# A three-stage attention kernel: new slot tables for all stages, three masks instead of four on TensorE, and whole-width first fills

## The reference

```python
# layer 0: grouped convolution (8 heads, kernel 3) makes q, k, v
scores = einsum('bhdl,bhdm->bhlm', qh, kh) / sqrt(8) - 1e9 * mask      # 8 heads, 256 keys, causal
x = layernorm(softmax(scores) @ vh + swapaxes(q_in))                   # B=128, L=256, C=128
# layer 1 (self) and layer 2 (keys and values from ctx): 16 heads of depth 16, 128 keys
logits = einsum('bhqd,bhkd->bhqk', qh, kh) / 4 + mask * -1e9
out = layernorm(x + (softmax(logits) @ vh) @ wo + bo)
# feed-forward 256 -> 1024 -> 256 with relu, residual and layernorm
```

## Time and profile before

| | us |
|---|---|
| median of 3 runs | 4481.46 (4481.1 to 4481.8) |
| the profiled execution | 4476.52 |
| its span on the core | 4474.7 |
| PE busy in the span | 4144.4 (93%) |
| DVE busy | 3523.3 (79%) |
| ACT, POOL busy | 3136.7 (70%), 2872.4 (64%) |

### The profile page before, as it was taken

How to read it: one execution, slowest core, us unless ns; L and a number is a source line. 1 busy time by engine, 2 the same in 40 slices (tenths; PEclk the granted TensorE clock), 3 DMA queues, 4 the chain that set the end, 5 groups by cost and what they waited for, 6 DMA issues and landing times. The chain is left out here.

```text
span 4474.7 us, 129562 instructions
## 1 busy us (share of the span) xinstructions
PE 4144.4 (93%) x46216; PEld 3376.6 (75%) x46216; DVE 3523.3 (79%) x13839; ACT 3136.7 (70%) x6279; POOL 2872.4 (64%) x4568
## 2 busy tenths in 40 slices
PE   7999999999999969999999986999999997999999
PEld 5777777777777747777777765788787776999998
DVE  7898988989988859999999985777777774555555
ACT  5777777777777748888888875777777775444443
POOL 4777777777776637777777764766766762444444
PEclk9999999999999979999999998999999998999999
DMA  5444444444444436767777756898889882222221
GB/s 137 119 125 119 123 123 120 125 120 122 122 121 123 114 94 154 169 160 172 162 165 170 162 131 144 195 197 193 194 197 193 194 184 90 71 71 71 71 71 53
DMA packets 1082953, 608.79 MB, mean 136 GB/s; under 512 B 64664, under 2 KB 1082056, under 8 KB 1082312
## 3 DMA queue, kind: packets, MB, share of 16 engines
q1 hardware_dynamic: 1071896, 595.70, 54.8%
q10 hardware_dynamic: 10416, 4.80, 0.5%
HBM read 175.66 MB, written 117.54 MB: 66 GB/s over the span
## 5 line engine op out<-in xcount | busy, mean ns | idle before, releaser
L1142 DVE CUSTOM_DVE_ANT_0 l_junk<-l_bank,mask 128x256 bf16<-128x256 f32 x2048 | 776.8, 418 | 47.6 <-PE l_bank L830 33.7
L995 ACT ACTIVATE mha_probs<-mha_bank 128x512 f32<-128x512 f32 x1024 | 611.3, 601 | 278.9 <-DVE mha_bank L1157 154.0
L995 ACT ACTIVATE l_probs<-l_bank 128x512 f32<-128x512 f32 x1024 | 604.6, 597 | 266.2 <-DVE l_bank L1157 258.8
L1157 DVE TENSOR_TENSOR l_bank<-l_bank,mask0t 128x512 f32<-128x512 f32 x768 | 530.5, 691 | 25.9 <-PE l_bank L862 22.4
L1142 DVE CUSTOM_DVE_ANT_0 mha_junk<-mha_bank,mask 128x128 bf16<-128x128 f32 x2048 | 462.3, 284 | 29.7 <-PE mha_bank L830 29.4
L830 PE MATMUL l_bank<-l_stack 96*128 96x256 bf16 x2048 | 385.2, 274 | 58.8 <-DMA l_stack<-l_parts 29.6
L830 PE MATMUL mha_bank<-mha_stack 96*128 96x128 bf16 (+1 forms) x4096 | 355.8, 221 | 79.2 <-DVE mha_max_parts L1142 48.0
L1557 ACT ACTIVATE ffn_hidden<-ffn_h,ffn_b_s 128x512 f32<-128x512 f32 x256 | 176.4, 689 | 354.8 <-PE ffn_h L1504 344.1
L862 PE MATMUL l_bank<-l_stack 99*128 99x128 bf16 x4096 | 403.1, 221 | 9.7 <-ACT l_probs L995 4.3
L1157 DVE TENSOR_TENSOR mha_bank<-mha_bank,mask1t 128x512 f32<-128x512 f32 x512 | 354.9, 693 | 71.2 <-PE mha_bank L862 66.1
L862 PE MATMUL mha_bank<-mha_stack 99*128 99x128 bf16 (+1 forms) x4096 | 395.8, 220 | 15.4 <-DMA mha_stack<-mha_max_rows 13.6
(11 more groups left out here) (197 smaller groups left out, 11430.0 us busy)
## 6 DMA issues: line engine op xcount, KB each, us to landing
mha_stack<-mha_parts SPq DMA_DIRECT2D x1536, 128.0 KB, 3.5
l_stack<-l_parts SPq DMA_DIRECT2D x1024, 64.0 KB
l_stack<-l_parts SPq DMA_DIRECT2D x256, 128.0 KB
rows_o<-mha_resid SPq DMA_DIRECT2D x64, 512.0 KB, 3.5
cols_o<-mha_y_t SPq DMA_DIRECT2D x128, 256.0 KB, 3.0
l_x_pad<-in_x SPq DMA_DIRECT2D x64, 256.0 KB, 3.3
l_c_pad<-in_ctx SPq DMA_DIRECT2D x64, 256.0 KB, 3.2
l_resid<-in_x_t SPq DMA_DIRECT2D x64, 256.0 KB, 3.2
```

Of the source, the lines that this page charges most:

```text
L995: nc.scalar.activation(probs[:, i % RING, :], tbank[i % 2][:, :], ACT.Exp).then_inc(att_exp, 1)
L1142: ins = nc.vector.tensor_tensor_reduce(out=junk[:, i % 2, cols], in0=sbank[i % 2][:, cols], in1=mask, scale=1.0, scalar=LOWEST, op0=ALU.ad ...
L1157: nc.vector.tensor_tensor(bank_, bank_, mask.unsqueeze(1).to_broadcast([P, 4, P]), ALU.add).then_inc(att_masked, 1)
```

## The change

It has three parts.

1. The slot tables of all three stages are new. In stage 0 a fourth mask (chunk 15) moves from PE to DVE, the scores come mostly one slot later, and both halves of the values are done whole in slot 0 and slot 2. In stage 1 score chunks 2 and 4 are one slot later and the second values are done whole in slot 5. In stage 2 the scores start two slots later and end in slot 18 instead of 16, the turn of the heads moves from slot 4j+5 to 4j+6, the turn of maxima of half 1 from slot 3 to slot 5 and that of half 0 from slot 9 to slot 12, the last projection from slot 11 to slots 11 and 12, one turn of y from slot 7 to slot 9, and `split_slot` from 14 to 13.
2. The first unit of each stage fills its stack by transfers over all 512 tokens: half as many of them, each twice as large. Its first score waits for all of them.
3. The counts of the semaphores follow.

```diff
 stage 0:
-        score=[2, 3, 4, 6, 7, 8, 10, 10, 11, 12, 12, 13, 14, 14, 15, 16],
+        score=[3, 4, 5, 7, 7, 8, 10, 10, 11, 12, 12, 13, 14, 15, 16, 18],
-        pe_masks=(4, 12, 14, 15),
+        pe_masks=(4, 12, 14),
-        work=[((0, 1), 'values', 1, 0),
+        work=[((0,), 'values', 1, 0),
-              ((9,), 'turn_y', -1, 3),
+              ((8,), 'turn_y', -1, 3),
-              ((13,), 'turn_y', 0, 0),
+              ((12,), 'turn_y', 0, 0),
 stage 1:
-        score=[4, 4, 6, 8, 8, 9, 11, 12, 12, 13, 13, 14, 15, 15, 17, 18],
+        score=[4, 4, 7, 8, 9, 9, 11, 12, 12, 13, 13, 14, 15, 15, 17, 18],
-              ((5, 6), 'values', 1, 1),
+              ((5,), 'values', 1, 1),
 stage 2:
-        score=[2, 2, 4, 4, 6, 6, 8, 8, 11, 11, 12, 13, 13, 14, 15, 16],
+        score=[4, 4, 5, 7, 8, 8, 9, 9, 10, 10, 12, 13, 13, 14, 15, 18],
-        steps={'turn': 5, 'turn_merged': 7, 'output': 8, 'normalise': 9},
-        dve_steps={'recip': (5, 1), 'merge': (5, 2), 'low': (7, 1), 'add': (8, 1), 'stats': (8, 1), 'moments': (9, 0), 'epsilon': (9, 1)},
+        steps={'turn': 6, 'turn_merged': 7, 'output': 8, 'normalise': 9},
+        dve_steps={'recip': (5, 1), 'merge': (5, 1), 'low': (6, 2), 'add': (8, 2), 'stats': (8, 2), 'moments': (9, 1), 'epsilon': (9, 1)},
         work=[((0,), 'values', 1, 0),
-              ((1,), 'values', 1, 1),
-              ((3,), 'max', 0, 1),
-              ((3, 4), 'project', 2, 0),
+              ((2,), 'values', 1, 1),
+              ((3,), 'project', 2, 0),
+              ((5,), 'max', 0, 1),
               ((6,), 'turn_y', -1, 2),
               ((7,), 'project', 2, 1),
-              ((7,), 'turn_y', -1, 3),
+              ((9,), 'turn_y', -1, 3),
               ((9,), 'project', 2, 2),
-              ((9,), 'max', 1, 0),
-              ((11,), 'project', 2, 3),
+              ((12,), 'max', 1, 0),
+              ((11, 12), 'project', 2, 3),
-        split_slot=14,
+        split_slot=13,
 the fills:
+        def fill_first(u, side):
+            fill_side(u, slice(0, 4 * P), stack_in[0][side], side)
```

More of the change, by code:

```diff
@@ L80 @@
         split_lag=0,
-        pool_steps={'power': (9, 0)},
+        pool_steps={'power': (9, 2)},
         work=[((0,), 'turn_y', -1, 1),
@@ L578, in attention, with filled @@
     FILLED = len(FILLS) + (1 if phase == 2 else 0)
+    FIRST_FILLED = [sum(sides[-1] == side for _, _, sides in FILLS) + (1 if phase == 2 and side == 0 else 0)
+                    for side in range(2)]
+    def filled(u, half):
+        return 16 * (FILLED * u.k + (FIRST_FILLED[half] if u.par == 0 else FILLED))
     def place(side, h):
@@ L680, in load_resid, with fill_side @@
                          res_units[u.u]).then_inc(resid_ld[u.par], 16)
-        def fill_side(u, half, side):
-            tokens = slice(2 * half * P, 2 * (half + 1) * P)
-            if side == 0:
-                wait(sp, att_mm, CHUNKS * (u.u - 2) + 8 * (half + 1) if u.number() not in (0, 1) else 0)
-                if phase == 2:
-                    sp.dma_start(stack[STACK:SCORED, u.par, side_of((1,)), tokens],
-                                 mask2_units[u.u][:, tokens].unsqueeze(1).to_broadcast([3, H, 2 * P])
-                                 ).then_inc(stack_in[u.par][half], 16)
+        def fill_side(u, tokens, signal, side):
+            if phase == 2 and side == 0:
+                sp.dma_start(stack[STACK:SCORED, u.par, side_of((1,)), tokens],
+                             mask2_units[u.u][:, tokens].unsqueeze(1).to_broadcast([3, H, tokens.stop - tokens.start])
+                             ).then_inc(signal, 16)
             wait(sp, split_done, projected(u, GROUPS * (side + 1) - 1))
@@ L695, in fill_side @@
                                  parts[:, u.par, GROUPS * sides[0]:GROUPS * (sides[-1] + 1), part, tokens]
-                                 ).then_inc(stack_in[u.par][half], 16)
+                                 ).then_inc(signal, 16)
+        def fill_first(u, side):
+            fill_side(u, slice(0, 4 * P), stack_in[0][side], side)
         def fill_stack(u, half):
-            fill_side(u, half, 0)
-            fill_side(u, half, 1)
+            wait(sp, att_mm, CHUNKS * (u.u - 2) + 8 * (half + 1) if u.number() != 1 else 0)
+            for side in range(2):
+                fill_side(u, slice(2 * half * P, 2 * (half + 1) * P), stack_in[u.par][half], side)
         def store(u):
@@ L737, in slots @@
             if t.number() == -2:
-                for half in range(2):
-                    fill_side(t.plus(2), half, 0)
+                fill_first(t.plus(2), 0)
             yield
@@ L747, in slots @@
             if t.number() == -2:
-                for half in range(2):
-                    fill_side(t.plus(2), half, 1)
+                fill_first(t.plus(2), 1)
             elif exists(t.plus(2), N):
@@ L822, in score_step @@
             if i % 8 == 0:
-                pe.wait_ge(stack_in[u.par][i // 8], 16 * FILLED * (u.k + 1))
+                for half in range(2) if u.number() == 0 else (i // 8,):
+                    pe.wait_ge(stack_in[u.par][half], filled(u, half))
             if i == 0 and phase == 2 and u.number() == 0:
@@ L959, in project_out @@
                 for half in range(2):
[L960 removed]
+                    act.wait_ge(stage1[f"stack_in0{half}"], c["stage1_filled"][half])
             if i == 0:
                 for half in range(2):
[L963 removed]
+                    wait(act, stack_in[u.par][half], filled(u.plus(-2), half))
             args = {"scale": SCALE if side == 0 else 1.0}
@@ L1373, in attention @@
         c["stage1_values"] = work_count(Unit(N // 2 - 1, 1), "values", VSTEPS - 1)
-        c["stage1_fills"] = 16 * FILLED
+        c["stage1_filled"] = [filled(Unit(N // 2 - 1, 0), half) for half in range(2)]
     return dict(n=N, sync=sync_program, tensor=tensor_program, scalar=scalar_program, vector=vector_program,
```

6 lines of the change are left out of this document (2 added, 4 removed).

## The result

| | before | after |
|---|---|---|
| median of 4 runs | 4481.63 (4481.1 to 4482.28) | 4563.55 (4558.58 to 4567.76) |
| the profiled execution | 4476.52 | 4558.58 |
| its span | 4474.7 | 4556.8 |
| mean granted clock | 0.985 | 0.974 |

The changed kernel is slower: ratio 1.0182, 95% interval 1.0165 to 1.02, 82 us. The forecast was 4542 us, with a range of 4455 to 4605. "0 to 1" is the distance from the first exponential of stage 0's last unit to that of stage 1's first.

What follows compares the result with a forecast made beforehand. PE's list was taken as the path in stages 0 and 2, PE and DVE bounding each other in stage 1. Terms -30 + 0 - 10 + 101 = +61 us, on 4476.5 plus 4.9, gave 4542 us; range 4455 to 4605.

Steps and rivals of the forecast that it cites:

- The cover from the rows of before: Stage 2: PE's work between the turn of maxima of half 1 and attend 8, 3.27 us after 8.84 before.
- the transfer (5.5): Stage 2: time from ACT's issue of the maxima transfer to attend 8, taken as 5.5 us, near the loaded rows.
- The wait forecast, 2.95 us a unit: Stage 2: new wait of PE at attend 8 for the transfer of maxima, 31 times, +91 us in all.
- The case of 6.08 us: Stage 2: slowest traced issue-to-attend time, which the prediction placed in the last unit; worst-case wait 3.53 us.
- The turn of the heads' wait: Stage 2: PE's 0.48 us wait at this turn goes, since it comes two slots behind the freeing output; -15 us.
- +0.4 us for each of the two: Stage 2: PE's waits for maxima (0.69 us) and normalisation (0.60 us) each grow by 0.4 us, 25 us together.
- a rival with 20%: Stage 2: the clock falls in each unit behind the wait, costing 1.7 us of PE's time, 53 us: 4595; chance 20%.
- Two matmuls off PE, 35.8 us less: Stage 0: leaving chunk 15's mask off PE saves 0.56 us in each of 64 units, 35.8 us.
- The fills' wait, 21.2 us: Stage 0: PE's 21.2 us of waiting for stack fills goes, since the first score comes one slot later.
- nothing else on PE changes its count there: Stage 0: apart from the mask's two matmuls, PE's work keeps its count; the stage's forecast was -30 us.
- DVE did not become the bound: Stage 0 rival: DVE, 0.69 us more a unit, becomes the bound; stage 0 +22 instead of -30, 4594; chance 12%.
- until SP gets to its end: Barrier into stage 2: PE stands still 16.70 us for SP's queue; issuing 13 instead of 26 saves 8.5 us.
- The other steps of PE and ACT are long done: Barrier into stage 2: no other chain ends later than SP's issues, so the 8.5 us less counts in full.

Runs made afterwards that it cites:

- experiment 4: Changed kernel, each of the 24 fills of stage 2's later units moving a quarter of its rows (32 KB instead of 128 KB): 4451.14 us, ratio 0.9935.
- Experiment 3: Changed kernel with ten further, unused matmuls of 512 columns on PE ahead of attend 8's wait for the maxima in stage 2: 4515.52 us, ratio 1.0083.
- experiment 9: Changed kernel with stage 2's old table, plus chunk 15's mask back on PE: 4465.05 us; or instead stage 0's turn of y back in slot 13: 4447.73 us.

## Why the prediction was right, and where it was wrong

**Stage 2, the transfer: right, both as cause and as size.** The cover from the rows of before (3.27 us) was 3.39, the turn to the issue (0.72) was 0.77, and the transfer (5.5) was 5.2. The wait forecast, 2.95 us a unit, is 2.6 to 2.7. The choice near the loaded end was the one that mattered, and experiment 4 shows its reason, the fills around it. (The case of 6.08 us that it leaned on is the last unit but one, with twelve fills around it, and not the last.) The Trainium skill's rule ("DMA: Bandwidth & Descriptors", section "Anatomy of one DMA — SWDGE (gpsimd) path"), an estimate of 2.06 us for 24 KB, is stated for one DMA on GpSimd's path, and this one goes from ACT's queue. No transfer that PE waited for in stages 1 and 2 was that fast in any trace: the shortest took 2.45 us, and 2.9 was the median with few bytes.

**Stage 2, the other waits.** The turn of the heads' wait went (-0.48), as forecast. The step that failed is "+0.4 us for each of the two": each time that it occurs, the wait for maxima went from 0.69 to 0.73 us and the one for the normalisation from 0.60 to 0.55. That PE's halt at attend 8 gives DVE time is not the reason, since in experiment 4, where the halt is gone, they are 0.74 and 0.55 (21.4 us in 29 and 15.3 us in 28 cases). The new order has the room that the forecast denied it; the 0.8 us a unit did not come.

**The clock.** It stood as a rival with 20% and 1.7 us a unit, in place of nothing in the sum. Experiment 3 measures 1.41 us. So the forecast of +3.27 a unit met +3.37 by luck, in offsetting errors: 0.8 us for waits that did not grow and a transfer's wait 0.3 us too large stood in for 1.4 us of clock. By experiment 3 the sum is 1.96 (32.30 - 30.34: the new wait less the old one of the heads) and 1.41. The argument against the rival, that no wait of the steady stages was over 1.5 us, said only that the trace of before could not show it; the step that failed is that it then put the clock at nothing in the sum.

**Stage 0.** -30 was forecast and -21 came, but not by its steps. "Two matmuls off PE, 35.8 us less" failed: experiment 9 gives 3 us for it. The rest, 18.7 us (1530.8 to 1512.1), comes with four masks still on PE. The fills' wait, 21.2 us, is gone there as forecast, but a wait of 39.0 us for the heads' copy is new. What makes up for it is PE's own time: 1386.29 of 1450 us at 24.00 us a unit are 22.95 us, against 1400.36 at 24.30, or 23.47, before, some 33 us in 63 units with the same matmuls. By the distances between their starts, without idle time, 0.26 us of it lie in the values (2.94 to 2.68 a unit) and 0.35 in scores and attends (8.05 to 7.70), and the others take 0.1 more. So "nothing else on PE changes its count there" is true and says nothing of its time. Which of the table's moves gives this was not tried alone (the table also moves one step of POOL, 'add', by a place). DVE did not become the bound; ACT's copy of y ahead of the heads' copy did, which the forecast did not see, since it followed DVE's list and not ACT's at the moved turn of y.

**Starts of stages.** -10 was forecast; fills alone give 0 (10 is outside the interval). The step that failed is "until SP gets to its end": PE's wait there is 16.54 us now and was 16.70, since the load of x, ACT's rounding and POOL's subtraction end last. "The other steps of PE and ACT are long done" left out POOL and ACT's rounding, and the larger fills make the load late.

**Stage 1.** 0 was forecast, -2 seen.

**The sum.** +61 against +82 in the two profiled executions: 9 us of the difference from stage 0, 10.4 from the starts, 3.5 from stage 2 and -2.1 from stage 1. The median of the changed kernel lies 5 us above its profiled execution, as it did before (4.9). That the total came within 21 us of the forecast is in part luck too: stage 2's errors offset each other, and those of stage 0 and of the starts, 19 us, add up.

## What to carry to other kernels

Before a small transfer that an engine waits for is moved, measure its time where other transfers are under way, and compare the engine's own work between cause and use with it: here the transfer took 5.2 us and 0.8 passed ahead of it, against 3.4 of work, while with a quarter of the fills' load it took 2.9. Look also at what stands ahead of the issue on the engine that issues it: in slot 3 that took 2.5 us instead of 0.8. If a wait for a DMA appears in each round of TensorE, price the half clock with it, and test the two apart with matmuls that fill the wait. Where several chains end at a barrier, the gain is at most the distance to the chain that ends last without the change, so follow every engine's last step there, ACT's and POOL's too.

## What the runs showed of the hardware

- More matmuls made the kernel 48 us faster: ten of 512 columns in each unit of stage 2, inside a wait of 2.6 us, took all 23 stretches at half clock away.
- A 24 KB transfer from ACT's queue took 2.9 us in the median with fills of 32 KB around it and 5.2 us with the same number of fills of 128 KB, 7.1 us at worst, although those are issued by SP.
- In stage 1, where PE waited for this transfer, it took 5.6 us in the median for half 1 and 3.9 for half 0 (10 and 12 cases in the changed kernel's trace). How the fills stand around it there is not shown.
- Twice as large fills (256 KB) took SP 0.76 us each to issue instead of 0.67, and the stores and loads behind them took longer to issue too: 5.25 us instead of 3.73.
